# A recurrent scan with an attention block behind it: the order of all pieces past the scan is replaced by another one

## The reference, cut to what matters

```python
def step(h, xt):
    m = concatenate([xt, h]) @ weight + bias
    g = sigmoid(m[:, :128] + 1.0); c = tanh(m[:, 128:])
    return g * h + (1 - g) * c
x = x + scan(step, cond, x)
xm = expmap0(layer_norm(logmap0(x)) * (1 + sc_msa) + sh_msa)
q, k, v = heads(plin(xm, w_q)), heads(plin(xm, w_k)), heads(plin(xm, w_v))   # 16 heads of 8
attn_out = plin(from_heads(softmax(q @ k.T / sqrt(8)) @ v), w_o)
r = mobius_add(x, expmap0(g_msa * logmap0(attn_out)))
xm = expmap0(layer_norm(logmap0(r)) * (1 + sc_mlp) + sh_mlp)
ff = plin(plin(xm, w_f1), w_f2)
y = x + mobius_add(r, expmap0(g_mlp * logmap0(ff)))
```

## Time and profile before

| | us |
|---|---|
| median of 3 runs | 487.18 (486.27 to 487.44) |
| the profiled execution | 487.77 |
| its span, first to last instruction | 485.5 |
| end of the scan in it | 314.7 |
| DVE busy, of the span | 318.4 |
| PE busy, of the span | 364.5 |

### The profile page before, as it was taken

One profiled execution on the slowest core, in us unless ns is written; L12 is line 12 of the kernel. 1 busy time (PEld: TensorE's weight loads), 2 busy tenths in 40 slices (PEclk: granted clock), 3 DMA queues, 4 the chain that ended last, 5 costly groups with the idle time before them and its releaser, 6 DMA issues.

```text
span 485.5 us, 14029 instructions
## 1 busy us (share of the span) xinstructions
PE 364.5 (75%) x5194; PEld 252.9 (52%) x5194; DVE 318.4 (66%) x1939; ACT 215.4 (44%) x963; POOL 141.0 (29%) x295
## 2 busy tenths in 40 slices
PE   2997987977666787668999989988499788745400
PEld 1746674656555665545665756646345455424400
DVE  6444444575886676886575687554823679798984
ACT  2224222323334323335545455546498886644410
POOL 6000000121480022380013084024700342554642
PEclk9999999999999999999999999999689969767565
DMA  7107500020000000000000000000000000000010
GB/s 176 54 1 158 107 3 1 2 46 2 1 2 3 1 2 3 2 2 1 2 3 3 3 1 2 3 2 1 2 3 1 1 2 2 2 22 3 6 38 22
DMA packets 9113, 8.41 MB, mean 17 GB/s; under 512 B 1275, under 2 KB 7693, under 8 KB 9046
## 3 DMA queue, kind: packets, MB, share of 16 engines
q1 hardware_dynamic: 8950, 7.26, 6.5%
q0 software_dynamic: 96, 0.26, 0.2%
HBM read 6.45 MB, written 1.08 MB: 15 GB/s over the span
## 4 chain that ended last, share of the span: by engine, by line
PE 53%; DVE 24%; ACT 12%; issue 5%; POOL 4%; DMA 1%; SPq 0%; DVEq 0%; POOLq 0%; ACTq 0%
PE zb L778 19%; PE tb L883 5%; DVE prod_hi L1388 4%; PE tb L729 4%; PE firsts L926 4%; PE zb L757 4%; ACT state L1141 3%; PE firsts L947 3%; DVE prod_lo L1394 3%; ACT prd L1274 2%; PE firsts L1019 2%; ACT state L1144 2%; PE zb L763 2%; POOL stat L679 2%; PE firsts L778 2%
## 5 line engine op out<-in xcount | busy, mean ns | idle before, releaser
L778 PEld LDWEIGHTS zb<-prod_hi,whh 128*128 128x128 f16 x1920 | 73.5, 106 | 94.5 <-DVE prod_hi L1388 87.0
L778 PE MATMUL zb<-prod_hi,whh 128*128 128x8 f16 x1920 | 90.7, 171 | 40.5 <-DVE prod_hi L1388 39.6
L1141 ACT ACTIVATE state<-zb 128x8 f32<-128x8 f32 x240 | 42.4, 177 | 168.3 <-PE zb L778 168.3
L1388 DVE SCALAR_TENSOR_TENSOR prod_hi<-state 128x16 f16<-128x16 f32 x255 | 47.3, 185 | 97.8 <-ACT state L1144 95.1
L778 PE MATMUL zb<-prod_lo,whh 128*128 128x8 f16 x960 | 63.5, 172 | 2.9 <-DVE prod_lo L1394 1.0
L1394 DVE TENSOR_TENSOR prod_lo<-prod,prod_hi 128x16 f16<-128x16 f32 x255 | 50.7, 199 | 8.7
L778 PEld LDWEIGHTS zb<-prod_lo,whh 128*128 128x128 f16 x960 | 44.4, 107 | 6.8 <-DVE prod_lo L1394 3.6
L588 POOL TENSOR_TENSOR stat<-mv 128x4 f32<-128x4 f32 x4 | 0.8, 205 | 155.8 <-DVE mv L1484 155.8
L1274 ACT ACTIVATE prd<-zb 128x640 f32<-128x640 f32 x64 | 41.1, 713 | 7.1 <-PE zb L998 6.9
L1390 DVE SCALAR_TENSOR_TENSOR prod<-state 128x16 f32<-128x16 f32 x256 | 43.8, 171 | 0.5 <-ACT state L1144 0.5
L1144 ACT ACTIVATE state<-zb 128x16 f32<-128x16 f32 x240 | 42.8, 178 | 0.0
(11 more groups left out here) (331 smaller groups left out, 726.5 us busy)
## 6 DMA issues: line engine op xcount, KB each, us to landing
mod<-ada_rows SPq DMA_DIRECT2D x4, 768.0 KB, 12.3
resid<-in_x_dram SPq DMA_DIRECT2D x6, 128.0 KB, 3.7
ffz<-shift_rows SPq DMA_DIRECT2D x4, 131.0 KB, 3.3
out_dram<-state SPq DMA_DIRECT2D x8, 64.0 KB, 2.1
out_dram<-early SPq DMA_DIRECT2D x8, 64.0 KB, 2.1
yy<-in_L_cond_w_ada_dram SPq DMA_DIRECT2D x1, 384.0 KB
early<-in_L_cond_weight_dram SPq DMA_DIRECT2D x2, 128.0 KB
resid<-in_x_dram POOLq DMA_DIRECT2D x2, 128.0 KB, 3.5
```

Source lines behind the costliest of these rows:

```text
L778: i = pe.matmul(z_bank(t, k)[:, NB * (t % CH):NB * (t % CH) + NB], whh[:, half, p, k, :], src[:, NB * p:NB * p + NB], start=False, stop=Fa ...
L1141: act.activation(r[:, 24:32], z_bank(t, 1)[:, k:k + NB], ACT.Tanh, scale=-1.0 / ZS)
L1388: dve.scalar_tensor_tensor(prod_hi[:, :], r[:, 16:32], 1.0, r[:, 0:16], ALU.add, ALU.mult).then_inc(hi_ready, 1)
```

## The change

The tables of ticks past the scan are all new. The code of the tails is rewritten for groups of tails (`PAIRS`): a piece's tick becomes a tuple with one entry for each tail of the group. The groups in use are single ones, `((0,), (1,), (2,), (3,))`, so every loop over a group runs once, the instructions of a tail and their waits stay the same, and the small scratch tiles `tmp` and `itmp` are laid out otherwise. In the code, `gy` stands behind `g` in a loop of its own; in the ticks of tail 0 `gy` is now behind `gdot` of its own tail. No instruction is added or taken away. The ticks of tails 0 to 2 under `out_`, and some single ones over 1560 (tail 3's `asq`, `ffsq`, `ffscale`, `add`, the last entries of `artanh_`), belong to pieces that don't exist.

The ticks of the pieces that matter below, for tails 0, 1, 2, 3 unless the name says otherwise:

| piece | before | after |
|---|---|---|
| ot | 537 662 868 1096 | 531 657 814 992 |
| wo | 598 711 979 1164 | 593 716 891 1051 |
| m | 617 734 995 1188 | 612 734 910 1070 |
| norm | 666 767 1039 1214 | 678 807 958 1091 |
| mob | 692 792 1061 1258 | 708 837 994 1127 |
| x2 | 723 835 1138 1312 | 760 871 1046 1158 |
| g | 810 928 1229 1395 | 873 1009 1164 1237 |
| gdot | 827 978 1248 1447 | 897 1021 1197 1251 |
| gy | 830 1018 1237 1412 | 933 1018 1181 1248 |
| clip3 | 912 1060 1299 1488 | 985 1243 1270 1364 |
| f2 | 931 1095 1323 1504 | 1117 1289 1300 1381 |
| norm3 | 971 1155 1358 1533 | 1286 1338 1380 1413 |
| mob2 | 1013 1181 1391 1540 | 1392 1400 1420 1443 |
| out | 1071 1363 1419 1575 | 1453 1465 1484 1504 |
| add | 1082 1379 1431 - | 1465 1484 1503 - |
| out_ of tail 3 (its two halves end) | 1581 1593 | 1519 1530 |
| first half of group 0, last half of group 31 (exps) | 371 1049 | 366 970 |
| saved, batches 3, 4, 5, 7 | 655 762 857 1083 | 650 745 807 985 |

The diff, cut to tables of two tails, the attention's first and last ticks, and the code around `gy`:

```diff
-    ot=(537, 559), o=(549, 570), oT=580, oevac=591, wo=598, m=617, wosq=643, asq=653, adot=625,
-    norm=666, tanh=690, mob=692, ascale=715, root=724, x2=723, v=752, vtrans=764, vevac=791,
-    vsq=795, artanh=768, lin=824, rho=825, t6=799, g=810, gy=830, gdot=827, usum=846, clip2=876,
-    fq=876, e=893, f1=904, clip3=912, y=911, f2=931, f2sq=942, ffsq=959, fdot=953, norm3=971,
-    fftanh=992, mob2=1013, ffscale=1062, out=1071, add=1082, artanh_=(773, 775, 777, 780, 782,
-    785, 787, 789, 791, 794, 798, 800, 803, 805, 807, 810, 815, 818, 821, 823, 778), mob_=(696,
-    699, 701, 704, 706, 708), ss_=(711, 716, 719, 722), usum_=(867, 871, 874), fq_=(886, 892,
-    890), f1_=(906, 908, 910), mob2_=(1017, 1023, 1026, 1044, 1046, 1058), ffm=944, o_=(553,
-    574), out_=(978, 980, 982))
+    ot=(531, 554), o=(544, 565), oT=(575,), oevac=(585,), wo=(593,), m=(612,), wosq=(638,),
+    asq=(666,), adot=(621,), norm=678, tanh=705, mob=708, ascale=(726,), root=761, x2=(760,),
+    v=(772,), vtrans=(804,), vevac=(818,), vsq=(823,), artanh=782, lin=(856,), rho=854,
+    t6=(841,), g=(873,), gy=(933,), gdot=(897,), usum=906, clip2=940, fq=940, e=(953,), f1=964,
+    clip3=985, y=(972,), f2=(1117,), f2sq=(1129,), ffsq=(1267,), fdot=(1342,), norm3=1286,
+    fftanh=1313, mob2=1392, ffscale=(1442,), out=(1453,), add=(1465,), artanh_=(787, 789, 791,
+    794, 797, 799, 801, 803, 805, 813, 815, 817, 818, 820, 822, 828, 845, 847, 850, 852, 1566),
+    mob_=(711, 714, 716, 719, 721, 723), ss_=(726, 731, 742, 759), usum_=(909, 935, 938),
+    fq_=(945, 951, 949), f1_=(966, 968, 970), mob2_=(1422, 1427, 1429, 1434, 1437, 1440),
+    ffm=(1260,), o_=(548, 569), out_=(1902, 1910, 1918))
...
-    ot=(1096, 1104), o=(1107, 1128), oT=1138, oevac=1158, wo=1164, m=1188, wosq=1203, asq=1216,
-    adot=1202, norm=1214, tanh=1236, mob=1258, ascale=1290, root=1315, x2=1312, v=1341,
-    vtrans=1352, vevac=1372, vsq=1376, artanh=1359, lin=1443, rho=1444, t6=1378, g=1395,
-    gy=1412, gdot=1447, usum=1455, clip2=1463, fq=1462, e=1470, f1=1480, clip3=1488, y=1487,
-    f2=1504, f2sq=1516, ffsq=1416, fdot=1523, norm3=1533, fftanh=1554, mob2=1540, ffscale=1488,
-    out=1575, add=1504, artanh_=(1373, 1376, 1377, 1380, 1383, 1386, 1394, 1397, 1399, 1402,
-    1404, 1406, 1409, 1411, 1413, 1414, 1416, 1418, 1430, 1432, 1330), mob_=(1261, 1265, 1268,
-    1272, 1274, 1287), ss_=(1290, 1295, 1309, 1310), usum_=(1457, 1459, 1461), fq_=(1464, 1469,
...
+    ot=(992, 1001), o=(1003, 1011), oT=(1026,), oevac=(1045,), wo=(1051,), m=(1070,),
+    wosq=(1079,), asq=(3574,), adot=(1081,), norm=1091, tanh=1118, mob=1127, ascale=(1146,),
+    root=1159, x2=(1158,), v=(1169,), vtrans=(1198,), vevac=(1215,), vsq=(1220,), artanh=1180,
+    lin=(1247,), rho=1259, t6=(1221,), g=(1237,), gy=(1248,), gdot=(1251,), usum=1277,
+    clip2=1313, fq=1312, e=(1331,), f1=1341, clip3=1364, y=(1362,), f2=(1381,), f2sq=(1393,),
+    ffsq=(4126,), fdot=(1403,), norm3=1413, fftanh=1440, mob2=1443, ffscale=(4214,),
+    out=(1504,), add=(4254,), artanh_=(1185, 1187, 1189, 1191, 1205, 1208, 1210, 1212, 1214,
+    1216, 1218, 1221, 1223, 1225, 1237, 1239, 1241, 1243, 1245, 1246, 3894), mob_=(1131, 1135,
+    1137, 1139, 1141, 1143), ss_=(1146, 1151, 1154, 1157), usum_=(1288, 1299, 1311), fq_=(1320,
...
-    scores=(364, 368, 379, 384, 391, 407, 409, 426, 428, 441, 447, 457, 458, 473, 475, 485, 491,
-    501, 503, 512, 518, 527, 529, 549, 550, 569, 570, 590, 591, 616, 617, 627, 633, 642, 644,
-    681, 682, 692, 704, 729, 730, 740, 746, 774, 780, 789, 791, 819, 821, 840, 844, 853, 857,
-    885, 886, 896, 902, 947, 948, 994, 995, 1005, 1034, 1045), exps=(371, 377, 383, 389, 396,
-    414, 420, 430, 436, 444, 450, 461, 467, 478, 484, 489, 495, 504, 510, 516, 522, 531, 537,
...
-    997, 1026, 1032, 1038, 1049), saved=(457, 513, 578, 655, 762, 857, 962, 1083), before=(19,
...
+    scores=(359, 363, 374, 380, 386, 402, 405, 421, 423, 438, 440, 452, 459, 468, 470, 480, 486,
+    496, 498, 507, 513, 522, 524, 544, 545, 564, 565, 585, 586, 611, 612, 622, 628, 637, 639,
+    656, 677, 686, 688, 707, 708, 733, 735, 745, 751, 760, 762, 779, 785, 794, 796, 833, 834,
+    862, 863, 883, 884, 909, 910, 929, 931, 950, 951, 965), exps=(366, 372, 379, 384, 391, 409,
+    415, 425, 431, 444, 450, 456, 462, 473, 479, 484, 490, 499, 505, 511, 517, 526, 532, 547,
...
+    940, 958, 964, 970), saved=(450, 508, 576, 650, 745, 807, 928, 985), before=(19, 24, 52, 57,
...
+PAIRS = ((0,), (1,), (2,), (3,))
...
-        tmp = sb("tmp", [P, 1 + NJ, 28, NC])
-        itmp = sb("itmp", [P, 1 + NJ, 2, NC], I32)
+        tmp = sb("tmp", [P, 28, NC + NT])
+        itmp = sb("itmp", [P, 2, NC + NT], I32)
...
+                        yield from at_ticks(now, base + T["g"][p])
+                        products(j, "g", T_OT[j], gw[:, 0:D]).then_inc(g_ps, 1)
+                    for p, j in enumerate(PAIRS[n]):
+                        yield from at_ticks(now, base + T["gy"][p])
+                        products(j, "gy", T_OT[j], gw[:, D:2 * D]).then_inc(gy_ps, 1)
```

More of the change, by code:

```diff
@@ L170 @@
 TURN = {use: n for n, use in enumerate(USES)}
-END = STEPS + max(max(t["out"], t["add"]) for t in TAILS) + 60
+END = STEPS + max(max(t["out"] + t["add"] + t["out_"]) for t in TAILS) + 60
 def att_groups():
@@ L719, in tail @@
                 return work
-            tails = [tail(j) for j in range(NJ)]
+            tails = [tail(n) for n in range(len(PAIRS))]
             run(lambda t: None, [tokens, *tails])
@@ L1078, in work @@
-                    yield from at_ticks(now, base + T["oT"])
-                    pe.wait_ge(o_ready, NC * j + NC)
-                    transposes("oT", T_O[j]).then_inc(oT_ps, 1)
-                    yield from at_ticks(now, base + T["wo"])
-                    pe.wait_ge(oT_sb, j + 1)
-                    pe.wait_ge(bo_split, 1)
-                    b = bank("wo")
-                    for half in range(2):
-                        pe.matmul(b, onesh[:, 0:P], boh[:, half].rearrange("p c d -> p (c d)"),
-                                  start=(half == 0), stop=False, skip_group_check=True)
@@ L1088, in work @@
-                    for c in range(NC):
-                        ins = pe.matmul(b[:, D * c:D * c + D], T_OT[j][:, c, :], wo_s[:, :], start=False,
-                                        stop=True, skip_group_check=True)
-                    ins.then_inc(wo_ps, 1)
-                    yield from at_ticks(now, base + T["vtrans"])
-                    pe.wait_ge(v_ready, j + 1)
-                    transposes("vT", T_O[j]).then_inc(vT_ps, 1)
-                    yield from at_ticks(now, base + T["t6"])
@@ L1096, in work @@
-                    pe.wait_ge(vT_sb, j + 1)
-                    b = bank("t6")
-                    for c in range(NC):
-                        ins = pe.matmul(b[:, 8 * c:8 * c + LIN], T_OT[j][:, c, :], lin[:, j, :],
-                                        start=(c == 0), stop=True, skip_group_check=True)
-                    ins.then_inc(t6_ps, 1)
-                    yield from at_ticks(now, base + T["g"])
-                    products("g", T_OT[j], gw[:, 0:D]).then_inc(g_ps, 1)
-                    yield from at_ticks(now, base + T["gy"])
@@ L1742, in work @@
                     dve.tensor_tensor(ss, e1, e3, ALU.add).then_inc(v_moments, 1)
-                    yield from at_ticks(now, base + T["x2"])
-                    for c in range(NC):
-                        x = T_X[j][:, c, :]
-                        dve.wait_ge(att_scaled, NC * j + c + 1)
-                        done_(dve.scalar_tensor_tensor(x, x1[:, c, :], st("aP", tok_tile(c, j)), x,
-                                                       ALU.mult, ALU.add))
-                    mark = done[0]
@@ L1764, in work @@
-                    for half in range(2):
-                        pp_ = slice(CH * half, CH * half + CH)
-                        ins = dve.tensor_copy(
-                            view(stat[pp_, k, NC * j:NC * j + 1], [NT, 3], [2, 2], [1, 2]),
-                            view(tail_bank(j, "t6")[pp_, half:half + 1], [2, 3], [16, 2],
-                                 [9 - 2 * half, 2]))
-                    ins.then_inc(v_lin, 1)
-                    yield from at_ticks(now, base + T["gdot"])
```

563 lines of the change are left out of this document (313 added, 250 removed), and 4 rows, old and new, of the table scores.

## The result

| | before | after |
|---|---|---|
| median, side by side on one chip | 486.79 (486.27 to 487.44, 4 runs) | 481.56 (481.39 to 481.89, 4 runs) |
| the profiled execution | 487.77 | 481.39 |
| its span | 485.5 | 479.1 |

The ratio of the two medians is 0.9893, 95% interval [0.9876, 0.991]: 5.2 us faster. 479.3 was predicted, in a range of 475.2 to 483.8, so the sign and the range hold and the point is 2.3 us too low.

The account below looks back on a forecast made before the run. DVE was taken as the bound from 427.85 us, with a latency chain at the end; 45 ticks of slip put the first store at 465.1, plus 9.7 and 2.8 gave span 477.6, median 479.3, range 475.2 to 483.8 us.

Parts of the forecast that it names:

- 3 + 2 + 17: Lateness in ticks of 0.1 us up to batch 7 saved: 3 at saved 3, 2 for tail 0's norm, 17 clock.
- Where the gain lies: Attention first, tails 0 to 2 late: fills 2.72 us of idle DVE at the end, part of 10.84 us before 427.85.
- nothing comes of it: Rival: attention ends about when it did, DVE's work is only done later; 485.7 to 488.6 us, chance 0.06.
- slower: Rival: half the clock for most of the attention; median 491 us at 60% of it, chance 0.06.
- the table held almost to the letter: Rival: the new ticks hold with slip 10 to 25; median 475.8 to 477.3 us, chance 0.16.
- the forecast's: Main case: slip 25 to 60 ticks, median 477.3 to 480.8 us, chance 0.52.
- the clock eats more: Rival: half-clock spells in the attention and late wo, g, t6 for tails 2 and 3; 480.8 to 485.8, chance 0.20.
- Start: Up to the scores: all ticks from scores on fall by 5, taken as 0.5 us, bounds 0 and 0.8.
- The clock in the attention: Up to batch 7 saved: half a half-clock spell, 17 ticks, bounds 0 and 57.
- The clock behind the attention: After the attention, PE thin and often at 1.2 GHz: late wo, t6 and g delay DVE 18 ticks, bounds 0 and 25.
- POOL: the step that failed: Late tails: POOL full, norms 2 ticks and clips one tick longer than the table; 5 ticks, bounds 0 and 12.
- The stores: At the end: sixteen stores in SP's queue, 0.65 us each, end the kernel, cost 3.2 us and hide the adds' delays.

Follow-up runs that it names:

- second profile: The changed kernel run and profiled again with no edit: 481.84 us, ratio 0.9895 to the kernel before.
- the filler: Changed kernel plus 58 identity products in TensorE's idle stretches between 416 and 437 us: 482.17 us, ratio 0.9903 to the kernel before.
- the cheap norms: Changed kernel with the power of the last norm of tails 0, 1 and 2 computed as a product: 478.53 us, ratio 0.984 to the kernel before.

## Why the prediction was nearly right, and which step was off

Slips in ticks at the marks, from each profile's own `hcopy` (first profile, second):

| term of the sum | predicted | measured |
|---|---|---|
| at saved 7: 3 + 2 + 17 | 22 | 27, 23 |
| phase behind it, to usum of tail 3 | 18 | 12, 7 |
| POOL: to f2 of tail 3, then to the first add | 5 | 24 + 6, 24 + 6 |
| at add of tail 0 | 45 | 68, 60 |
| from that add to the end (1.4 + 9.7 + 2.8) | 13.9 us | 13.98, 13.99 |

- **Where the gain lies: right.** The attention ended 14.8 us earlier (413.02, named near 413.5), the granted clock over it was 0.95 (above 0.85 named), and `mob2` of tails 0 to 2 filled the last tail's norm. The rivals "nothing comes of it" and "slower" are out; so is the table held almost to the letter (slip 10 to 25). One argument against "slower" was misread: of the two half-clock spells of the old attention the first lasted some 10 us, the second (414.9 to 421.7) only 7.
- **Which case came: not the forecast's.** The slips of 68 and 60 and the median of 481.56 lie in the range of the rival "the clock eats more" (60 to 110, 480.8 to 485.8), above the forecast's 477.3 to 480.8. But the clock did not eat most of them (below).
- **Start: wrong by 0.6 and 1.0 us.** The first exponential came 36.85 us after `hcopy`, 36.77 before (351.51 less 314.74); the 0.5 us of the ticks did not arrive. At `saved` 3 the slip was 9 and 13, not 3.
- **The clock in the attention: too large.** 17 ticks were taken. A half-clock spell costs 8, and eight of twelve profiles had none. `saved` 3 to 7 was 18 and 10 ticks late, against 19 in the sum: 10 of them are there with the clock at 1.00 throughout, and no run says what they are. That the slip at `saved` 7 came out at 27 and 23 for 22 is therefore luck: the start and these 10 ticks made up for the clock.
- **The clock behind the attention: too large, and its cause did not act.** 18 ticks were for late `wo`, `g` and `t6`; 12 and 7 came. The clock was as slow as feared (0.72 over the stretch), yet DVE waited for PE only once for more than 0.5 us, 0.56 at `gdot` of tail 3, and in the second profile not at all for more than 0.3; keeping the clock up by the filler won nothing.
- **POOL: the step that failed.** "POOL is full from 1243 to 1438 and its norms are 2 ticks longer than the table's 27, its clips one: 5, bounds 0 and 12." It was 30, and 24 of them before `f2` of tail 3, beyond the bound of 12. By its own sizes 5 was too little, as four norms of 2 ticks each stand in one full queue. The sizes, taken from the earlier trace rows, were those of a norm standing alone: here the four took 4.2, 3.2, 3.3 and 3.1 us, and 1.0 of the first is the pair of products beside DVE's. The excess of each that stands ahead of `clip3` of tail 3 is handed on in POOL's queue to DVE's `f2`, and the ring with ACT adds to it: undoing one link of it gave 0.7 and 0.5. With the cheap norms 2.3 of the 2.4 us of that stretch went away. So DVE, which the prediction named as the bound with no idle stretch over 1 us, was not the bound there. The last 6 ticks, up to the first add, are there in that run too (8.97): DVE is busy 8.34 of 8.95 us and idle 0.60 at `mob2` of tail 3, whose norm that run left whole and which took 3.1 us where the table has 2.7:

```profile
462.82 0.16 DVE L1639 TENSOR_TENSOR tmp<-stat 128x4 f32<-128x4 f32 x1 [0.60 <-ACT stat L1348]
```

- **The stores: right.** 13.9 us predicted from the add to the end, 13.98 measured; 3.2 us for SP's queue, and a second queue gave back 2.6. The adds were hidden behind it: 1.0 us each for four products of DVE (1.0 to 1.3 named), not the whole 1.26 to 1.38 of the add, and 2.3 us came off once SP's queue was halved and they were cut.
- **The total.** 68 less 45 ticks is 2.3 us late, 0.94 of the early scan end is to be taken off: 1.4, and the span was 479.1 against the 477.6 of the sum. The median was 481.56, where 0.6 had been taken off the profiled time; here the profiled time was 0.2 below the median, so another 0.8 came from there.

## What to carry to other kernels

When pieces are packed closer, cost the small serial engine by its queue and not by its instruction: write down which in-order queue stands behind each late piece, add up what each piece takes in the crowd, and follow the waits until they close, as here from POOL over ACT's squares back to POOL and on to DVE. Count stretches from the last event that the change can't touch, as the same code ahead of it moved by 1.8 us between executions. And where many outputs become ready together, count the issuing queue first: sixteen stores on one queue cost 2.6 us, which a second engine's queue took back; when the outputs came faster still, the second queue was the next bound.
